# Edge tiles gathered once each, dense layers between the last steps of a segment sum, on one core of a Trainium2 chip

## The chip, the cores and the metric

The kernel runs on one NeuronCore of a Trainium2 chip (trn2). A core has five engines with an instruction queue each: TensorE (PE, with its weight loads as PEld) for matrix products, VectorE (DVE) and ScalarE (ACT) for elementwise work, GpSimd (POOL), which here issues the indirect DMAs, and SyncE (SP), which issues plain DMAs. The metric is the device time of one execution in microseconds. Before the change it is 7244.13 us, the median of 3 runs (7237.43 to 7245.76).

## The reference, cut to what matters

A graph of 6250 nodes with 128 features and 100000 edges, sorted by destination `dst`, goes through four blocks, each a layer norm, a graph layer and a residual:

```python
msg = h[src] * norm[:, None]                        # block 1: three GCN layers, ReLU after each
out = jax.ops.segment_sum(msg, dst, num_segments=n) + b
# norm = dis[src] * ew * dis[dst], dis = rsqrt(degree), self loops added to the edges

agg = segment_sum(edge_weight[:, None] * x[src], dst); out = x + agg    # block 2 (GIN)
h = relu(out @ W1 + b1);  return h @ W2 + b2

score = (softmax_dst(qs*k) + softmax_dst(qd*k) + softmax_dst(qs*qd)) * distance ** lam  # block 3
h = segment_sum(score[..., None] * v[dst], dst);  leaky_relu(h @ Wo.T + bo)

agg = segment_sum(x[src], dst) / max(deg, 1)        # block 4 (SAGE)
out = agg @ W_l.T + b_l + x @ W_r.T;  return out / norm(out)
```

## The kernel before

**Tiles, blocks and steps.** The edges lie in `NT` = 782 tiles of 128. The nodes lie in `NB` = 49 blocks of 128, taken in `NGR` = 13 groups of up to four. A tile whose edges reach into several blocks must be summed once for each. The kernel makes a plan on the chip from `dst`: a list of steps, each a pair of a tile and a block. It has room for `NS` = 832 steps (782 + 48, rounded up to a multiple of 16). The plan (`plan_reg`) gives the block of each step, the first edge of its tile, and columns with a column for every step: `rel_col` (the place of each edge in its block), `ew_col` (its weight), `src_col` (its source node).

**A pass** is one segment sum over all edges. There are five: three for the GCN layers, one for GIN, one for SAGE. For each of the 832 steps:

- POOL (`gathers`, L627) issues an indirect DMA that fetches the 128 source rows of the step from a table in HBM into a slot of `gath_ring` (64 slots, slot = step modulo 64). From step 64 on, a slot is written again when the product that read it has signalled `freed`, which every eighth product does.
- DVE (`sums`) waits for a batch of four gathers, makes the one-hot matrix of the step (L1347: which edge goes to which node, times the weight) in `hot_ring`, and six steps later adds the product to the block (L1358). The block's place in `AGG` comes from a register that a load from `plan_reg` fills for 16 steps at a time. Each add waits for the one before it.
- PE (`products`) runs `KEEP_BUSY` = 3 products of no use to the result (L749, 128x512 bf16, on a bank of their own), waits for the one-hot matrix, and multiplies it by the gathered rows (L751, f32; the trace shows two matmuls for each). The products go round seven PSUM banks.

**Between the passes** stand dense layers (`dense`, PE): per group four transposes (L726), a copy of the turned group by ACT (L947, in `dense_copies`), four products with the weights (L740), and DVE's read of the result from PSUM (`drained`). Turn g+1 stands ahead of product g. Before GCN layers 1 and 2 DVE also multiplies the sums by `dis` and adds the bias (`bias_add`, L1056), and a turn waits for that. The result goes to `Y` (L1067), SP stores it group by group to the table in HBM, and POOL copies it to `AGG` (L591), where the next sums start from the nodes' own rows. The first gather of a pass waits until all 13 stores have landed. After the third pass DVE scales and biases (L1075), adds the residual (L1078) and does the next norm; after the fifth it multiplies the sums by `inv_cnt` (L1129), and finishes the rows (L1151, L1153, L1155, L1138, L1140), which SP stores to `out`.

**Attention** (block 3) stands between the fourth and fifth pass. It too takes the 832 steps, with gathers of its own (L609) from the same `src_col`. **The setup** of some 387 us makes the plan and columns: seven gathers of edge fields (L571), casts and masks on DVE, transposes (PE) and copies (L1254) into the columns, degrees.

## Time and profile before

| | before |
|---|---|
| median of 3 runs | 7244.13 us (7237.43 to 7245.76) |
| profiled execution, its own time | 7238.71 us |
| its span | 7236.9 us |
| granted TensorE clock, mean | 0.962 of full speed |
| PE busy | 5333.0 us (74%) |
| POOL busy | 5036.9 us (70%) |
| DVE busy | 3802.8 us (53%) |
| ACT busy | 1178.4 us (16%) |

The span is the time from the first to the last instruction; the execution's own time is 1.8 us longer. Busy shares are means over passes, dense stages, setup and attention, which have different limits. The clock is given as a share of 2.4 GHz: 1.00 is 2.4 GHz and 0.50 is 1.2 GHz. Issuing instructions and the small instructions that compute addresses from registers are not counted as busy. A row of the timeline may merge several instructions, and the time in it is then their common stretch.

### The profile page before, as it was taken

To read this page: it belongs to the slowest core of one execution; us is meant where nothing else is said; L and a number is where in the kernel's file an instruction comes from. 1 tells how busy PE (TensorE), PEld (TensorE's weight loads), DVE (VectorE), ACT (ScalarE), POOL (GpSimd) and SP (SyncE) were. 2 spreads that over 40 slices of the span, in tenths; PEclk is the share of its full clock that TensorE was granted. 3 is DMA by queue.
4 is the path that set the end of the run, shared out by engine and by line. 5 is a ranking of instruction groups with operands and counts; after the bars stand their busy time and mean duration, and the time that the engine had idled before them with its cause. 6 is when DMAs were issued, how large, how long until landed. Compare 5 with 4: busy or idle time off the path is not lost.

```text
span 7236.9 us, 99962 instructions
## 1 busy us (share of the span) xinstructions
PE 5333.0 (74%) x30048; PEld 3426.1 (47%) x30467; DVE 3802.8 (53%) x12655; ACT 1178.4 (16%) x3122; POOL 5036.9 (70%) x5072
## 2 busy tenths in 40 slices
PE   0677777777777777777667777779999984777776
PEld 0444444444444444444344444556666663444444
DVE  7934444444444434444544444468988987333335
ACT  0600000000000000000000000057777773000000
POOL 7067777677777677777567777657777761777774
PEclk9599999999999999999999999989999996999999
DMA  1022222222222222222222222146666650222221
GB/s 51 17 63 53 53 53 53 53 61 53 53 53 53 57 57 53 53 53 53 53 56 53 53 53 53 45 109 142 145 144 144 145 124 24 53 53 53 53 53 51
DMA packets 390629, 481.00 MB, mean 66 GB/s; under 512 B 106605, under 2 KB 292879, under 8 KB 390075
## 3 DMA queue, kind: packets, MB, share of 16 engines
q0 software_dynamic: 160528, 330.23, 18.3%
q1 hardware_dynamic: 226395, 143.05, 8.4%
q8 instruction: 244, 4.00, 0.2%
q14 instruction: 294, 2.41, 0.1%
q10 hardware_dynamic: 3168, 1.31, 0.1%
HBM read 449.69 MB, written 26.88 MB: 66 GB/s over the span
## 4 chain that ended last, share of the span: by engine, by line
POOL 56%; issue 20%; PE 10%; DVE 7%; DMA 5%; SPq 1%; ACT 1%; ACTq 0%; POOLq 0%; DVEq 0%
POOL pool L627 54%; DMA gath<-table,src_col 2%; DMA pool<-edge_attr 2%; DVE pool L1222 2%; POOL gath L609 2%; PE psum L660 1%; PE psum L792 1%; PE psum L783 1%; PE psum L776 1%; PE psum L818 1%; PE psum L740 1%; SPq L527 1%; PE psum L769 1%; PE psum L762 1%; DVE hot L1314 0%
## 5 line engine op out<-in xcount | busy, mean ns | idle before, releaser
L627 POOL DMA_INDIRECT pool<-table,src_col x4160 | 3932.9, 945 | 1439.2 <-issue 1266.3
L749 PE MATMUL psum<-busy_rows,iota_b 128*128 128x512 bf16 x12061 | 3303.3, 381 | 22.3 <-issue 0.4
L751 PE MATMUL psum<-pool 128*128 128x128 f32 x8320 | 1715.0, 288 | 1378.7 <-DVE pool L1347 1378.4
L751 PEld LDWEIGHTS psum<-pool 128*128 128x128 f32 x8320 | 1505.1, 191 | 2345.1 <-DVE pool L1347 1892.5
L1347 DVE TENSOR_SCALAR pool<-iota_f,rel_col,ew_col 128x128 f32<-128x128 f32 x3328 | 1242.1, 375 | 2289.7 <-DMA pool<-table,src_col 2288.7
L749 PEld LDWEIGHTS psum<-busy_rows,iota_b 128*128 128x128 bf16 x12480 | 1235.2, 99 | 546.0 <-issue 8.8
L1358 DVE TENSOR_TENSOR work<-work,psum 128x128 f32 x4160 | 1193.1, 287 | 251.9 <-PE psum L751 225.4
L609 POOL DMA_INDIRECT gath<-table,src_col x832 | 906.9, 1090 | 267.9 <-issue 220.4
L947 ACT ACTIVATE pool<-psum 128x512 f32<-128x512 f32 (+1 forms) x130 | 72.1, 566 | 4278.0 <-PE psum L726 4277.9
L1347 DVE TENSOR_SCALAR pool<-iota_f,rel_col 128x128 f32<-128x128 f32 x832 | 250.2, 302 | 577.9 <-DMA pool<-table,src_col 577.4
L818 PEld LDWEIGHTS psum<-pool,hot 128*128 128x128 f32 x1664 | 221.9, 198 | 120.4 <-issue 109.7
L783 PE MATMUL psum<-pool,weights 128*128 128x512 f32 x416 | 239.7, 659 | 0.0
L776 PE MATMUL psum<-pool 128*128 128x128 f32 x1664 | 234.9, 287 | 0.0
L792 PE MATMUL psum<-pool,head_sum 128*32 128x512 f32 x1248 | 233.3, 638 | 0.5 <-DVE pool L1379 0.5
L818 PE MATMUL psum<-pool,hot 128*128 128x72 f32 x1664 | 222.5, 276 | 8.8 <-DVE work L1443 5.7
L928 ACT ACTIVATE ln_rstd<-ln_rstd 128x4 f32<-128x4 f32 (+1 forms) x52 | 10.6, 204 | 1333.0 <-DVE ln_rstd L1321 1333.0
L776 PEld LDWEIGHTS psum<-pool 128*128 128x128 f32 x1664 | 216.2, 203 | 0.0
L1374 DVE TENSOR_TENSOR pool<-psum,pool 128x512 f32<-128x512 f32 x208 | 142.0, 683 | 128.6 <-PE psum L792 121.8
L769 PE MATMUL psum<-ident,gath 128*128 128x128 f32 x832 | 142.2, 282 | 69.2 <-DMA gath<-table,src_col 68.8
L964 ACT ACTIVATE pool<-QV 128x128 f32 x832 | 189.5, 298 | 12.7 <-DVE pool L1451 5.6
L740 PE MATMUL psum<-weights,pool 128*128 128x128 f32 x980 | 145.3, 298 | 45.4 <-ACT pool L947 44.3
L1377 DVE SCALAR_TENSOR_TENSOR pool<-psum,bk_col,pool 128x512 f32<-128x512 f32 x208 | 154.2, 741 | 27.2 <-PE psum L783 26.7
(195 smaller groups left out, 3769.2 us busy)
## 6 DMA issues: line engine op xcount, KB each, us to landing
pool<-table,src_col POOLq DMA_INDIRECT x4160, 2.5
pool<-edge_attr SPq DMA_DIRECT2D x832, 64.0 KB
pool<-step_masks SPq DMA_DIRECT2D x624, 48.0 KB
pool<-rel_rows SPq DMA_DIRECT2D x208, 128.0 KB
table<-work SPq DMA_DIRECT2D x60, 256.0 KB, 2.3
gath<-table,src_col POOLq DMA_INDIRECT x832
table<-QV SPq DMA_DIRECT2D x12, 256.0 KB, 2.3
out<-X SPq DMA_DIRECT2D x12, 256.0 KB
```

Of the source, the lines that this page charges most:

```text
L609: gp.indirect_dma_start(out=q_src[:, n % SLOTS, :], out_offset=None, in_=table[0][:, :], in_offset=bass.IndirectOffsetOnAxis(ap=src_col[:, ...
L627: gp.indirect_dma_start(out=gath_ring[:, s % RING, :], out_offset=None, in_=source[:, :], in_offset=bass.IndirectOffsetOnAxis(ap=src_col[: ...
L740: ins = pe.matmul(psum[:, 4 + g % 2, i * P:(i + 1) * P], tr[:, 2 * k + g % 2, i * P:(i + 1) * P], weights[:, WI[w], :], start=(k == 0), st ...
L749: pe.matmul(psum[:, SUM_BANKS, :], iota_b[:, :], busy_rows[:, :], start=True, stop=True)
L751: pe.matmul(psum[:, s % SUM_BANKS, 0:D], hot_ring[:, s % HOT_RING, :], gath_ring[:, s % RING, :], start=True, stop=True).then_inc(steps.pr ...
L769: pe.transpose(psum[:, B_QS, j * P:(j + 1) * P], q_src[:, n % SLOTS, :], ident[:, :]).then_inc(qsrc_turned, 1)
L776: pe.matmul(psum[:, B_QD, j * P:(j + 1) * P], q_block[:, n % SLOT2, :], expand[:, two, j * P:(j + 1) * P], start=True, stop=True).then_inc ...
L783: pe.matmul(psum[:, B_K, :], weights[:, WI["Wk"], :], attr_t[:, g % 2, :], start=True, stop=True).then_inc(keyed, 1)
L792: ins = pe.matmul(psum[32 * kind:32 * (kind + 1), bank, :], head_sum[:, q, :], prod[:, kind, :], start=(q == 0), stop=(q == QUADS - 1), ti ...
L818: ins = pe.matmul(psum[:, B_SUM, q * ACCW:(q + 1) * ACCW].rearrange("p (k i h) -> p k i h", k=3, i=KINDS), hot[:, two * QUADS + q, :], val ...
L1347: v.tensor_scalar(hot_ring[:, s % HOT_RING, :], iota_f[:, :], rel_col[:, s:s + 1], ew_col[:, s:s + 1] if weighted else None, ALU.is_equal, ...
L1358: v.tensor_tensor(into, into, psum[:, a % SUM_BANKS, 0:D].rearrange("p (a d) -> p a d", a=1), ALU.add).then_inc(steps.added, 1)
```

## The change

- `gathers` loops over the 782 tiles instead of the 832 steps, from a `src_col` that has a column for every tile. A step finds its tile's slot by a third row of the plan (tile modulo 64), from which PE loads registers for 16 steps at a time. DVE waits for tile s before step s, for the first 782 steps; the last 48 steps (`PS` = 830 steps are left) wait for no gather. A gather of tile t waits for the product of step t-13 (`slot_free`), and every fourth product signals `freed`.
- `KEEP_BUSY` is 2, and the last 48 steps have none.
- A block b is complete once 782 + b steps are added. So the turns and products of the dense layers of GCN 1 and 2, GIN 1 and SAGE stand between the last steps (`then`), a stage every four steps from step 788, and DVE's reads of them a read every four steps from step 796. After the third pass, DVE's residual and norm stand there from step 788. What is not through by the last step follows it.
- The last 48 steps use banks 7, 6, 2, 3 (SAGE: 7, 6), since the dense stages take the others. An add stands seven steps behind its one-hot matrix, four steps in the last 48 (SAGE: two).
- The add takes `dis` of the block (SAGE: `inv_cnt`) as a factor, in place of L1056, L1075's factor and L1129. The GCN biases of layers 0 and 1 are columns (`gcn_bias`) that ACT's copy of the turned group adds; the third is added in `gcn_out`.
- ACT, not POOL, sets `AGG` to the nodes' own rows, times `dis` (`gcn_start`: 49 activations of 128x128 a layer).
- The setup makes both layouts of the sources: three more loads, a cast, two more groups of transposes and copies, and two stores to HBM. SP loads the layout by steps before attention, and that by tiles after it.

```diff
-        FREE = 8
+        FREE = 4
-        KEEP_BUSY = 3
+        KEEP_BUSY = 2
...
+            def slot_free(self, t):
+                steps = t + FREE - 1 - RING + NB - 1 + 1
+                return self.nth * (PS // FREE) + ceil_div(steps, FREE) if steps > 0 else 0
+            def bank(self, s):
+                return s % SUM_BANKS if s < NT else self.tail_banks[(s - NT) % len(self.tail_banks)]
+            def lead(self, s):
+                return (SUM_BANKS if s < NT else len(self.tail_banks)) - 1
+            def group_added(self, g):
+                return self.before + NT + groups[g][1] - 1
+        passes = [Pass(i, (7, 6, 2, 3)) for i in range(4)] + [Pass(4, (7, 6))]
...
             for layer in range(3):
-                for g, (lo, hi) in enumerate(groups):
-                    gp.wait_ge(gcn[layer].drained, gcn[layer].before + g + 1)
-                    gp.tensor_copy(AGG[:, lo:hi, :], Y[:, lo:hi, :]).then_inc(gcn_started, 1)
                 gathers(gp, layer, table[layer % 2], passes[layer])
...
-            for s in range(NS):
-                if s % FREE == 0 and s >= RING:
-                    gp.wait_ge(steps.freed, (steps.before + s - RING) // FREE + 1)
+            for t in range(NT):
+                if t % FREE == 0 and t >= RING - NB:
+                    gp.wait_ge(steps.freed, steps.slot_free(t))
                 gp.indirect_dma_start(
...
+            dense(pe, gcn[0], [AGG], ["W0"], lambda g: pe.wait_ge(norm_x.normed, norm_x.before + g + 1))
+            products(pe, passes[0], dense_stages(pe, gcn[1], [AGG], ["W1"], complete(passes[0])))
+            products(pe, passes[1], dense_stages(pe, gcn[2], [AGG], ["W2"], complete(passes[1])))
+            products(pe, passes[2])
+            products(pe, passes[3], dense_stages(pe, gin_1, [AGG], ["G1"], complete(passes[3])))
...
+            products(pe, passes[4], dense_stages(pe, sage_dense, [AGG, Y], ["Wl", "Wr"], complete(passes[4])))
...
+            def stage_at(k):
+                if k < NGR:
+                    turn(k)
+                if k >= 1:
+                    multiply(k - 1)
...
+            for s in range(PS):
+                if s % REGS == 0:
+                    slots = load_plan(mybir.EngineType.PE, 2, s, REGS, RING - 1, "the plan takes the tile modulo RING")
+                if s < NT:
+                    for _ in range(KEEP_BUSY):
+                        pe.matmul(psum[:, SUM_BANKS, :], iota_b[:, :], busy_rows[:, :], start=True, stop=True)
                 pe.wait_ge(steps.hot, steps.before + s + 1)
...
+                          gath_ring[:, bass.ds(slots[s % REGS], 1), :].rearrange("p a d -> p (a d)"), start=True,
                           stop=True).then_inc(steps.product(s)[0], 1)
+                if then and s >= NT + STAGE_AT and (s - NT - STAGE_AT) % GROUP == 0:
+                    then.pop(0)()
...
+            def gcn_start(layer, g):
+                act.wait_ge(gcn[layer].drained, gcn[layer].before + g + 1)
+                for b in range(lo, hi):
+                    ins = act.activation(AGG[:, b, :], Y[:, b, :], ACT.Copy, scale=dis[:, b:b + 1])
...
+            def gcn_out(g):
+                v.wait_ge(passes[2].added, passes[2].group_added(g))
+                v.tensor_tensor(AGG[:, lo:hi, :], AGG[:, lo:hi, :], bias_of("b2", hi - lo), ALU.add)
...
+            for s in range(PS + SUM_BANKS):
+                while added < PS and (s >= PS or added < s - steps.lead(s)):
...
+                        v.scalar_tensor_tensor(into, part, scale[:, bass.ds(blocks[added % REGS], 1)], into, ALU.mult,
+                                               ALU.add).then_inc(steps.added, 1)
+                    added += 1
+                if s < PS:
+                    if s < NT and s % BATCH == 0:
+                        v.wait_ge(batch_here[s // BATCH % NBATCH], batch_value(steps.nth, s))
...
+                    if s >= NT + then_at and (s - NT - then_at) % GROUP == 0:
+                        then(groups_done)
+                        groups_done += 1
+            for g in range(groups_done, NGR):
+                then(g)
```

The order of the instructions shows three places. First DVE at the end of the first pass, before: the last adds (L1358; "ISA" computes the block's address from the register and carries the waits), then scale and bias (L1056) and the reads of the dense products (L1067).

```order
L1358 ISA [waits pass_added,pass_freed]
L1358 TENSOR_TENSOR work<-work,psum 128x128
L1056 SCALAR_TENSOR_TENSOR work<-work,dis,bias 128x128 [waits pass_added]
L1056 SCALAR_TENSOR_TENSOR work<-work,dis,bias 128x128 x11
L1067 TENSOR_TENSOR work<-psum,dis 128x512 [waits dense_multiplied]
L1056 SCALAR_TENSOR_TENSOR work<-work,dis,bias 128x128 x4
L1067 TENSOR_TENSOR work<-psum,dis 128x512 [waits dense_multiplied]
```

The same place now: four adds in a row where the last 48 steps begin, then an add (L1446) and a one-hot matrix (L1452) in turn, and after each four such pairs a read of a dense product (L1151).

```order
L1446 ISA [waits pass_added,pass_multiplied]
L1446 SCALAR_TENSOR_TENSOR work<-psum,dis,work 128x128
L1446 ISA [waits pass_added,pass_multiplied]
L1446 SCALAR_TENSOR_TENSOR work<-psum,dis,work 128x128
L1452 TENSOR_SCALAR pool<-iota_f,rel_col,ew_col 128x128
...
L1452 TENSOR_SCALAR pool<-iota_f,rel_col,ew_col 128x128
L1151 TENSOR_TENSOR work<-psum,dis 128x512 [waits dense_multiplied]
L1446 ISA [waits pass_added,pass_multiplied]
L1446 SCALAR_TENSOR_TENSOR work<-psum,dis,work 128x128
L1452 TENSOR_SCALAR pool<-iota_f,rel_col,ew_col 128x128
```

L1056 is gone, and L1151, which is the old L1067, stands between steps. Second PE, in the last steps of the first pass, before: fillers (L749), product (L751), then the dense layer's turns (L726) and products (L740).

```order
L749 MATMUL psum<-busy_rows,iota_b 128x512 x3
L751 MATMUL psum<-pool 128x128 [waits pass_hot]
L726 MATMUL psum<-ident,work 128x128 [waits gcn_biased]
L726 MATMUL psum<-ident,work 128x128 x3
L726 MATMUL psum<-ident,work 128x128 [waits gcn_biased]
L726 MATMUL psum<-ident,work 128x128 x3
L740 MATMUL psum<-weights,pool 128x128 [waits dense_drained,dense_copied]
L740 MATMUL psum<-weights,pool 128x128 x3
```

And now, from the last step with fillers (L824) on; L826 is the product, whose slot comes from a register, L788 the turn and L800 the dense product.

```order
L824 MATMUL psum<-busy_rows,iota_b 128x512 x2
L826 ISA [waits pass_hot]
L826 MATMUL psum<-pool 128x128
L826 ISA [waits pass_hot]
L826 MATMUL psum<-pool 128x128
...
L788 MATMUL psum<-ident,work 128x128 [waits dense_copied,pass_added]
L788 MATMUL psum<-ident,work 128x128 x3
L800 MATMUL psum<-weights,pool 128x128 [waits dense_copied]
L800 MATMUL psum<-weights,pool 128x128 x3
L826 ISA [waits pass_hot]
L826 MATMUL psum<-pool 128x128
```

A stage of the dense layer now stands behind every fourth product, and a product behind it waits for the stage. Third POOL, in the piece of the difference that holds the first passes:

```order
-L591 COPY work<-work 128x512 x12
-L591 COPY work<-work 128x128
-L627 DMA pool<-table,src_col 128x128 x832
-L591 COPY work<-work 128x512 x12
-L591 COPY work<-work 128x128
-L627 DMA pool<-table,src_col 128x128 x1664
+L685 DMA pool<-table,src_col 128x128 x3128
```

The copies are gone, and four passes now have 3128 = 4 x 782 gathers in one row.

## Rows read from the trace of the kernel before

**Rows 1.** The page: the chain that ended last, shares of the span.
```profile
POOL 56%; issue 20%; PE 10%; DVE 7%; DMA 5%; SPq 1%; ACT 1%; ACTq 0%; POOLq 0%; DVEq 0%
```

**Rows 2.** The page, groups by line: count, busy us, mean ns, idle before.
```profile
L627 POOL DMA_INDIRECT pool<-table,src_col x4160 | 3932.9, 945 | 1439.2 <-issue 1266.3 <-DMA table<-work 172.9
...
L1358 DVE TENSOR_TENSOR work<-work,psum 128x128 f32 x4160 | 1193.1, 287 | 251.9 <-PE psum L751 225.4 <-issue 11.9 <-DVE work L1358 6.2
```

**Rows 3.** Timeline of POOL, passes' ends and starts: start, us, instruction, idle before.
```profile
1426.39 0.94 POOL L627 DMA_INDIRECT pool<-table,src_col  x1 [0.30 <-issue]
...
1463.53 0.97 POOL L627 DMA_INDIRECT pool<-table,src_col  x1 [1.91 <-DMA table<-work]
...
2539.88 0.97 POOL L627 DMA_INDIRECT pool<-table,src_col  x1 [2.19 <-DMA table<-work]
...
3635.06 0.94 POOL L627 DMA_INDIRECT pool<-table,src_col  x1 [55.54 <-DMA table<-work]
...
7166.77 0.94 POOL L627 DMA_INDIRECT pool<-table,src_col  x1 [0.30 <-issue]
```

**Rows 4.** Timeline within one batch of four steps, DVE and PE.
```profile
909.80 0.34 DVE L1347 TENSOR_SCALAR pool<-iota_f,rel_col,ew_col 128x128 f32<-128x128 f32 x1
...
910.22 0.38 PE L751 MATMUL psum<-pool 128*128 128x128 f32 x2
...
910.30 0.34 DVE L1347 TENSOR_SCALAR pool<-iota_f,rel_col,ew_col 128x128 f32<-128x128 f32 x1
...
911.09 0.39 PE L751 MATMUL psum<-pool 128*128 128x128 f32 x2
```

**Rows 5.** Timeline of the first pass's last batch, and of the dense layer's end.
```profile
1429.05 0.35 DVE L1347 TENSOR_SCALAR pool<-iota_f,rel_col,ew_col 128x128 f32<-128x128 f32 x1 [3.03 <-DMA pool<-table,src_col]
...
1429.45 0.49 PE L751 MATMUL psum<-pool 128*128 128x128 f32 x2 [1.34 <-DVE pool L1347]
...
1434.15 0.29 DVE L1358 TENSOR_TENSOR work<-work,psum 128x128 f32 x1 [0.21 <-DVE work L1358]
...
1457.43 0.66 PE L726 MATMUL psum<-ident,work 128*128 128x128 f32 x4 [0.45 <-DVE work L1056]
```

**Rows 6.** Timeline: GIN's second layer starts; SAGE's first group.
```profile
4699.67 1.04 PE L726 MATMUL psum<-ident,work 128*128 128x128 f32 x8
...
7180.47 1.04 PE L726 MATMUL psum<-ident,work 128*128 128x128 f32 x8
7180.67 0.69 DVE L1151 TENSOR_TENSOR pool<-psum,bias 128x512 f32<-128x512 f32 x1 [4.16 <-PE psum L740]
7181.34 1.95 PE L740 MATMUL psum<-weights,pool 128*128 128x128 f32 x16
```

**Rows 7.** Groups by form, of what the change moves or alters.
```profile
L934 ACT ACTIVATE work<-X,ln_shift,ln_rstd 128x128 f32<-128x128 f32 x196 | 79.4, 481 | 2.5
...
L871 ACT ACTIVATE weights<-psum 128x128 f32<-128x128 f32 x6 | 1.7, 278 | 4.2 <-PE psum L695 4.2
...
L1056 DVE SCALAR_TENSOR_TENSOR work<-work,dis,bias 128x128 f32<-128x128 f32 x98 | 33.8, 407 | 0.1
L1067 DVE TENSOR_TENSOR work<-psum,dis 128x512 f32<-128x512 f32 x36 | 24.7, 686 | 21.0 <-PE psum L740 20.9
...
L1075 DVE SCALAR_TENSOR_TENSOR work<-work,dis,bias 128x128 f32<-128x128 f32 x49 | 14.0, 347 | 0.0
```

**Rows 8.** Timeline of PE where a batch came late in the first pass.
```profile
914.90 0.68 PE L751 MATMUL psum<-pool 128*128 128x128 f32 x2 [1.91 <-DVE pool L1347]
...
916.65 0.63 PE L751 MATMUL psum<-pool 128*128 128x128 f32 x2
```

**Rows 9.** Windows: stretch, length, busy us of PE PEld DVE ACT POOL, PEclk, DMA.
```profile
912.00:914.00 2.00, 0.99 (x6) 0.36 (x4) 0.00 (x0) 0.00 (x0) 1.39 (x3) 1.00 0.15 43
...
916.00:918.00 2.00, 2.00 (x8) 1.05 (x6) 0.54 (x4) 0.00 (x0) 1.43 (x2) 0.50 0.18 45
```

**Rows 10.** Timeline of the setup's longest step and of the first dense layer.
```profile
68.44 124.00 DVE L1222 TENSOR_SCALAR pool<-pool,base_of 128x128 f32<-128x128 f32 x7
...
209.31 1.15 DVE L1254 CAST src_col<-psum 128x512 int32<-128x512 f32 x2
...
373.41 0.69 DVE L1067 TENSOR_TENSOR work<-psum,dis 128x512 f32<-128x512 f32 x1 [0.64 <-PE psum L740]
```

More of the change, by code:

```diff
@@ L424, in build @@
         REGS = 16
+        STAGE_AT = 6
+        DRAIN_AT = 14
         def sync(sp):
@@ L727, in turn, with multiply @@
                     ins.then_inc(d.turned, 1)
-            turn(0)
-            for g, (lo, hi) in enumerate(groups):
-                if g + 1 < NGR:
-                    turn(g + 1)
+            def multiply(g):
+                lo, hi = groups[g]
                 pe.wait_ge(d.copied, d.before + (g + 1) * K)
@@ L1122, in vector @@
             settle()
-            sums(v, 4, passes[4], False)
-            def mean(g):
-                lo, hi = groups[g]
-                if g == 0:
-                    v.wait_ge(passes[4].added, passes[4].before + NS)
-                v.tensor_tensor(AGG[:, lo:hi, :], AGG[:, lo:hi, :], col_bc(inv_cnt, lo, hi), ALU.mult).then_inc(mean_made, 1)
             def result(g):
@@ L1140, in result, with sage_drain @@
                 v.tensor_tensor(X[:, lo:hi, :], X[:, lo:hi, :], st, ALU.add).then_inc(result_made, 1)
-            mean(0)
-            mean(1)
-            for g, (lo, hi) in enumerate(groups):
+            def sage_drain(g):
+                lo, hi = groups[g]
                 n = hi - lo
@@ L1159, in vector @@
                     result(g - 1)
-            result(NGR - 1)
+                if g == NGR - 1:
+                    result(g)
+            sums(v, passes[4], None, inv_cnt, DRAIN_AT, sage_drain)
         def product_of(g):
@@ L1338, in norm_feed, with sums @@
                 norm_end(v, norm, g)
[L1340 removed]
+        def sums(v, steps, weight, scale, then_at, then):
             v.wait_ge(plan_loaded, 16)
[L1343 to L1359 removed]
@@ new lines, in sums @@
+            added, groups_done = 0, 0
+            for s in range(PS + SUM_BANKS):
+                while added < PS and (s >= PS or added < s - steps.lead(s)):
+                    if added % REGS == 0:
+                        blocks = load_blocks(mybir.EngineType.DVE, added, REGS)
+                    v.wait_ge(*steps.product(added))
+                    if added >= 1:
+                        v.wait_ge(steps.added, steps.before + added)
+                    into = AGG[:, bass.ds(blocks[added % REGS], 1), :]
+                    part = psum[:, steps.bank(added), 0:D].rearrange("p (a d) -> p a d", a=1)
+                    if scale is None:
+                        v.tensor_tensor(into, into, part, ALU.add).then_inc(steps.added, 1)
+                    else:
+                        v.scalar_tensor_tensor(into, part, scale[:, bass.ds(blocks[added % REGS], 1)], into, ALU.mult,
[4 more added lines that the diff above has]
+                        v.wait_ge(batch_here[s // BATCH % NBATCH], batch_value(steps.nth, s))
+                    v.tensor_scalar(hot_ring[:, s % HOT_RING, :], iota_f[:, :], rel_col[:, s:s + 1],
+                                    weight[:, s:s + 1] if weight is not None else None, ALU.is_equal,
+                                    ALU.mult if weight is not None else ALU.bypass).then_inc(steps.hot, 1)
+                    if s >= NT + then_at and (s - NT - then_at) % GROUP == 0:
+                        then(groups_done)
+                        groups_done += 1
```

198 lines of the change are left out of this document (110 added, 88 removed).

## The prediction, made before the changed kernel was timed

> **What bounds the kernel now.** I read the chain of waits first. Its largest share is POOL, with "issue" behind it [rows 1]. The groups by line say what that is: 4160 gathers of 0.945 us, and 1266 us in which POOL waited for nothing but its own next issue, 0.30 us for each [rows 2]. So a gather costs 1.25 us, and a pass is 832 x 1.25 = 1040 us of them. DVE's adds wait on PE and its one-hot matrices on the gathers; neither sets the pace: within a batch DVE needs 0.50 us for a pair of matrix and add, and PE, at full clock with three fillers, 0.87 us a step [rows 4].
>
> POOL's timeline then shows what lies between passes [rows 3]. The first pass's last gather ends at 1427.33, and the next pass starts at 1463.53: a gap of 36.2 us. Pass 2 is like it (start to start 1076.3 us). After pass 3 the gap is 55.5 us. Pass 4's last gather should end at 3635.06 + 1040 = 4675.1, and what comes next there, GIN's second layer, starts at 4699.67 [rows 6], 24.6 us later. After the last gather of all (7167.71) 69.2 us remain of the span of 7236.9 us.
>
> The sum is made against the profiled execution, 7238.7 us; its span is 1.8 us shorter, and the median of the runs is 5.4 us longer, 0.07%.
>
> **Removed: 50 gathers a pass.** 50 x 1.25 = 62.5 us, five times: 312 us. They are steps whose tile is there already, and two of padding. Attention keeps its 832.
>
> **Added: 48 steps after the last gather.** They did lie under gathers; now they lie behind them. From the last gather's end:
> - 1.7 us until the first one-hot matrix of the last batch (1427.33 to 1429.05 [rows 5]).
> - Two pairs, 1.1 us. Then four adds in a row where one stood, since an add now follows by four steps and not seven: three more at 0.50 us, which is what chained adds take (0.29 + 0.21 of waiting for the last one [rows 5]), 1.5 us.
> - 48 pairs. The pair was 0.50 us [rows 4]. The add becomes a scalar_tensor_tensor with a factor read through a register. That form took 0.407 and 0.347 us on other operands [rows 7], against the add's 0.287 [rows 2], so a pair lies between 0.50 and 0.62 us. I take 0.55, nearer to the pair that was seen: 26.4 us.
> - Three more chained adds at the end, 1.5 us.
>
> Together 32.2 us a pass.
>
> **Moved: the dense layers of GCN 1 and 2.** Nine of 13 reads stand between the steps, at 0.69 us [rows 7]: 6.2 us. A PE stage is four turns and four products, 0.66 us [rows 5] and about 1.1 us, and the four step products 0.2 us each (0.87 less three fillers of 0.215). That is 2.6 us, against DVE's 4 x 0.55 + 0.69 = 2.9 us for the same four steps. PE just fits under DVE, but each waits for the other once a group; I allow 0.3 us of the waiting each time, 2.7 us (bounds 0 and 1.5 us each). The last groups stay uncovered: from the last full turn at 1457.43 to the first gather of the next pass at 1463.53 took 6.1 us [rows 3, 5]; with ACT's new work in between I take 6.5. The first stages run at half clock (below), 2.5 us. Sum 32.2 + 6.2 + 2.7 + 6.5 + 2.5 = 50.1 us where 62.5 + 36.2 = 98.7 us were: **48.6 us less, twice**.
>
> **GIN's first layer**: the same, without ACT's rows and the store at the end, 47.1 us where 62.5 + 24.6 = 87.1 us were: **40 us less**.
>
> **After pass 3** DVE bounds the gap before and now. Of its 55.5 us the first 7.1 are the adds' end (to 1434.44 in the first pass [rows 5]), and 48.4 the residual, norm and store. The factor goes into the add, so that per group a plain bias add of 0.69 us stands for four of 0.347 us with their starts overlapped: 5 us less over 12 groups. 32.2 + 43.4 = 75.6 us where 118.0 were: **42 us less**. PE is not needed in that stretch but for products.
>
> **SAGE.** Two banks, so an add follows its matrix by two: matrix to product 0.40 us, product 0.49 [rows 5], then add 0.25; a pair can't be under 0.60 us. 48 x 0.60 = 28.8; ahead of them 1.7 + 1.1 + 6 chained adds, 3.0. PE's stages are 1.04 + 1.95 us [rows 6] and lie beside DVE's 3.9 us of work a group, but for the first two: 5 us. DVE's own work is that from 7180.67 to the end, 56.2 us [rows 6], less 11 of the multiplications by `inv_cnt` at the 0.69 us of that form [rows 7], 48.6 us. Half clock 2.5 us. Sum 90.7 us where 62.5 + 69.2 = 131.7 us were: **41 us less**.
>
> **Setup.** DVE's cast of the second layout stands ahead of L1222, whose 124 us end at 192.4 whatever comes before [rows 10]: hidden. Two more copies of a column group are on the path, 1.1 us [rows 10]. The stores and loads of the layouts are waited for long after they land. In the first dense layer ACT gets four activations a group beside the copy of 0.6 us. They take 0.278 us (plain copy) to 0.481 us (with two column operands) [rows 7]; at 0.35 us ACT's period is 2.0 us, and the layer's was 1.33 us (0.69 + 0.64 of waiting [rows 10]). So ACT bounds this layer: 0.67 x 11 = **7.5 us more** (bounds 2 and 14). That POOL no longer copies gives nothing: the gathers wait for the stores.
>
> Sum: 2 x 48.6 + 40 + 42 + 41 = 220 us less, 8.6 us more: 7238.7 - 211.6 = 7027 us; with half of what the median lies above, **7030 us**.
>
> **The clock with two fillers.** A batch is 5.0 us of gathers. PE's work in it was 4 x 0.87 = 3.5 us and becomes 4 x 0.65 = 2.6 us, so that it idles some 2.4 us in each (two fillers of the next step run ahead of the wait). In the trace one batch came late and PE idled 1.91 us [rows 8]; the clock, 1.00 till then, was 0.50 right after and steps took 1.75 us until it came back [rows 8, 9]. So I expect 0.50 for part of every batch, and a mean well under 0.96. At 0.50 a step with two fillers is 1.75 - 0.43 = 1.32 us, a batch 5.3 us: PE is then never idle, and the clock comes back as it did here. The gathers wait for a product 13 tiles back, 16.2 us, and that product is through some 2.5 + 5.3 us after its gather was issued. The pass keeps its 1.25 us; only the tails start slow, which is in the sum with 2.5 us each. The Trainium skill, page "TensorE: Matmul & The Clock Gate", section "HAM oscillation — how this bites in real kernels", has the rule: where short bursts of matmuls alternate with waits for transfers, the clock falls in each wait and every burst starts cold. By it the sum stands; without it the four terms of 2.5 us would go and the time be 7020 us. The trace agrees, by that one late batch.
>
> **Rivals.**
> - *The last steps are bound by handshakes.* Every step is matrix, product, add across two engines, PE's stages stand in its queue before products that DVE waits for, and each product has a register instruction ahead of it that carries the wait. If a group costs the sum of both engines' work rather than the longer, 1.5 to 2 us come on 9 groups in three passes and 3 us on 9 in SAGE, and pairs go to 0.7 us: 45 + 27 + 36 = 108 us, 7138 us. For it: chained adds show 0.21 us of pure waiting [rows 5]. Against: four matrices are always ahead.
> - *PE becomes the bound, slower than before.* If PE stayed at 0.50, with 1.32 us a step and the register instruction on top, the 3910 steps would cost more than their gathers. The point from which this decides is 211.6 / 3910 = 0.054 us over 1.25: a mean step above 1.304 us is slower than before. At 1.38 us: 3910 x 0.13 = 508 us more, 7535 us. For it: two fillers, and 1.32 is above that point. Against: in the trace continuous work brought the clock back within two steps or so, and a PE that bounds is continuously busy.
> - *The ring stalls the gathers.* The lead was 64 tiles and is 13. Late batches and a slow PE could meet in it. Against: 16.2 us against 7.8. If a twentieth of a microsecond a gather came of it, 195 us, nearly all would be gone: 7225 us, with both signs about; a milder form, a third of that, gives 7095 us.
> - That the change doesn't do what it says is excluded by the order: 782 gathers a pass.
>
> **How the numbers follow.** Forecast 0.80, handshakes 0.11, PE bound 0.04, ring 0.05. The bounds: pair 0.50 to 0.62, waiting 0 to 1.5 us, ACT 2 to 14 us, half clock 0 to 5 us a tail give about 45 us below and 60 us above; toward the handshakes the range goes on somewhat: 6985 to 7105 us. A measurement of this kernel tells 0.2%, 14 us, from no change. Faster: the forecast, the handshakes, and most of the ring, 0.94; same 0.01; slower 0.05.
>
> **What would show it.** Right: the gathers at 1.25 us still, 782 of them a pass, and a start to start of some 1028 us (1076.3 now) in the first two passes and 1053 us (1095.2) in the third; no wait of POOL for PE; a mean clock clearly below 0.962; the first dense layer's reads 2.0 us apart. Wrong: gathers that wait for products; adds in the last steps over 0.7 us apart; a PE that has no idle time within the batches.

## The result, and the profile after

The changed kernel takes 7045.85 us (median of 4 runs, 7039.36 to 7051.43) where the kernel before, on the same chip, takes 7244.94 us (4 runs, 7237.43 to 7245.95): ratio 0.9727, 95% interval [0.971, 0.9744]. Forecast were 7030 us in a range of 6985 to 7105. The profiled execution took 7039.36 us, with a span of 7037.6 us and a mean granted clock of 0.87 (0.962 before).

The page of the kernel after: the chain of waits, then groups by line. They answer to [rows 1, 2].

```profile
POOL 47%; issue 19%; PE 13%; DVE 9%; DMA 8%; SPq 2%; ACT 1%; DVEq 1%; ACTq 0%; POOLq 0%
```

```profile
L685 POOL DMA_INDIRECT pool<-table,src_col x3910 | 3697.8, 946 | 1638.3 <-issue 1149.8
...
L1446 DVE SCALAR_TENSOR_TENSOR work<-psum,dis,work 128x128 f32 x2490 | 870.4, 350 | 140.3 <-PE psum L826 114.3
```

There are 3910 gathers of 0.946 us for 4160 of 0.945, still 0.30 us apart: the pace is the same and 250 are gone. Most of the idle time before them that "issue" did not end lies where the passes begin. The add with the factor takes 0.350 us; GIN, which has no factor, keeps the plain add of 0.287. The timeline of POOL shows the new gaps, against those of [rows 3].

```profile
1417.23 0.95 POOL L685 DMA_INDIRECT pool<-table,src_col  x1 [48.15 <-DMA table<-work]
...
2443.32 0.94 POOL L685 DMA_INDIRECT pool<-table,src_col  x1 [49.33 <-DMA table<-work]
...
3502.29 0.94 POOL L685 DMA_INDIRECT pool<-table,src_col  x1 [81.56 <-DMA table<-work]
```

The first gather of all starts at 392.16, so that start to start the first three passes take 1025.1, 1026.1 and 1059.0 us; 1028 us for the first two and 1053 us for the third were forecast, and before they took 1076.3 and 1095.2 us. The same readings for each part of the span, in us:

| part | before | after | change | forecast |
|---|---|---|---|---|
| setup, to the first gather | 387.2 | 392.2 | +4.9 | +8.6 |
| gathers of the five passes | 5199.2 | 4887.8 | -311.4 | -312 |
| gap after pass 1 | 36.2 | 48.2 | +12.0 | +13.9 |
| gap after pass 2 | 36.3 | 49.3 | +13.1 | +13.9 |
| gap after pass 3 | 55.6 | 81.6 | +26.0 | +20.1 |
| pass 4's end to attention | 70.8 | 88.0 | +17.2 | +22.5 |
| attention, to the first gather of pass 5 | 1382.5 | 1395.5 | +13.0 | 0 |
| SAGE, last gather to the end | 69.2 | 95.1 | +25.9 | +21.5 |

Without attention the span changes by -212.3 us, and -211.6 was forecast. The 13.0 us of attention were not forecast, and are most of what the median lies above 7030. The table compares one trace with one: before_again, below, is a second trace of the kernel before, with a setup of 391.5 us and an attention of 1393.1 us, so part of those two rows is variation.

The waits of POOL (what, releaser: us in all, times, longest) show that the ring held: a gather that waits for a product does so for 0.3 us, which is what it would have waited for its issue.

```profile
POOL pool L685 <- issue: 1149.8, 3773, 0.3
...
POOL pool L685 <- PE psum L826: 40.2, 132, 0.3
```

A window of a pass (length; PE, PEld, DVE, ACT, POOL busy; then the clock) shows the lower clock. Microsecond by microsecond it is 0.50 from 1000 to 1002 and from 1010 to 1012 us, and 1.00 from 1003 to 1009 and from 1013 us on: it falls after some of the waits within the batches, not after all. DVE's timeline of the first dense layer shows that its reads are 1.65 us apart, where 2.0 was forecast and 1.33 was before [rows 10].

```profile
1000.00:1020.00 20.00, 15.32 (x69) 9.56 (x68) 9.55 (x34) 0.00 (x0) 15.12 (x17) 0.85 0.22 55
```

```profile
377.12 0.69 DVE L1151 TENSOR_TENSOR work<-psum,dis 128x512 f32<-128x512 f32 x1 [0.90 <-PE psum L800]
378.77 0.69 DVE L1151 TENSOR_TENSOR work<-psum,dis 128x512 f32<-128x512 f32 x1 [0.96 <-PE psum L800]
```

### The profile page after: what moved, and what is told of

Read it like the earlier page. It is cut to its first block, busy times and chain, and to the rows that moved or that the text cites. A ratio compares the mean times of both kernels' runs of the same rounds, so it can differ in the third digit from the quotient of the medians.

```text
span 7037.6 us, 95131 instructions
## 1 busy us (share of the span) xinstructions
PE 5024.6 (71%) x25794; PEld 3266.4 (46%) x25794; DVE 4005.6 (57%) x12494; ACT 1222.8 (17%) x3269; POOL 4769.8 (68%) x4783
## 4 chain that ended last, share of the span: by engine, by line
POOL 47%; issue 19%; PE 13%; DVE 9%; DMA 8%; SPq 2%; ACT 1%; DVEq 1%; ACTq 0%; POOLq 0%
POOL pool L685 47%; DMA pool<-table,src_col 3%; DMA pool<-edge_attr 3%; DVE work L1308 2%; DVE work L1446 2%; PE psum L872 2%; PE psum L863 2%; PE psum L856 2%; PE psum L718 1%; PE psum L826 1%; PE psum L898 1%; SPq L584 1%; PE psum L800 1%; DMA gath<-table,src_col 1%; PE psum L842 1%
## 5 line engine op out<-in xcount | busy, mean ns | idle before, releaser
L685 POOL DMA_INDIRECT pool<-table,src_col x3910 | 3697.8, 946 | 1638.3 <-issue 1149.8
L826 PE MATMUL psum<-pool 128*128 x8300 | 1966.0, 326 | 1468.2 <-DVE pool L1452 1457.4
L826 PEld LDWEIGHTS psum<-pool 128*128 128x128 f32 x8300 | 1711.0, 223 | 2699.5 <-issue 2419.7
L824 PE MATMUL psum<-busy_rows,iota_b 128*128 128x512 bf16 x7820 | 2767.3, 441 | 67.8 <-issue 67.7
L1452 DVE TENSOR_SCALAR pool<-iota_f,rel_col,ew_col 128x128 f32<-128x128 f32 x3320 | 1243.6, 376 | 1967.4 <-DMA pool<-table,src_col 1966.4
L664 POOL DMA_INDIRECT gath<-table,src_col x832 | 898.8, 1080 | 287.6 <-issue 220.9
L1446 DVE SCALAR_TENSOR_TENSOR work<-psum,dis,work 128x128 f32 x2490 | 870.4, 350 | 140.3 <-PE psum L826 114.3
L824 PEld LDWEIGHTS psum<-busy_rows,iota_b 128*128 128x128 bf16 x7820 | 863.6, 112 | 183.6 <-issue 90.3
L1452 DVE TENSOR_SCALAR pool<-iota_f,rel_col 128x128 f32<-128x128 f32 x830 | 264.8, 320 | 484.1 <-DMA pool<-table,src_col 484.1
L1044 ACT ACTIVATE pool<-psum,gcn_bias 128x512 f32<-128x512 f32 (+1 forms) x26 | 17.2, 661 | 2005.7 <-PE psum L788 2005.7
L1446 DVE SCALAR_TENSOR_TENSOR work<-psum,inv_cnt,work 128x128 f32 x830 | 291.1, 351 | 73.0 <-PE psum L826 44.9
L1444 DVE TENSOR_TENSOR work<-work,psum 128x128 f32 x830 | 238.0, 287 | 48.4 <-PE psum L826 40.1
L856 PE MATMUL psum<-pool 128*128 128x128 f32 x1664 | 240.4, 292 | 0.0
L856 PEld LDWEIGHTS psum<-pool 128*128 128x128 f32 x1664 | 222.6, 208 | 0.0
L842 PE MATMUL psum<-ident,pool 128*128 128x128 f32 x832 | 150.5, 289 | 64.5 <-DMA pool<-edge_attr 61.0
```

The source lines that it names most:

```text
L664: gp.indirect_dma_start(out=q_src[:, n % SLOTS, :], out_offset=None, in_=table[0][:, :], in_offset=bass.IndirectOffsetOnAxis(ap=src_col[:, ...
L685: gp.indirect_dma_start(out=gath_ring[:, t % RING, :], out_offset=None, in_=source[:, :], in_offset=bass.IndirectOffsetOnAxis(ap=src_col[: ...
L824: pe.matmul(psum[:, SUM_BANKS, :], iota_b[:, :], busy_rows[:, :], start=True, stop=True)
L826: pe.matmul(psum[:, steps.bank(s), 0:D], hot_ring[:, s % HOT_RING, :], gath_ring[:, bass.ds(slots[s % REGS], 1), :].rearrange("p a d -> p ...
L842: pe.transpose(psum[:, B_ATTR, j * P:(j + 1) * P], attr[:, n % SLOT2, :], ident[:, :]).then_inc(attr_turned, 1)
L856: pe.matmul(psum[:, B_QD, j * P:(j + 1) * P], q_block[:, n % SLOT2, :], expand[:, two, j * P:(j + 1) * P], start=True, stop=True).then_inc ...
```

## The experiments

Twelve kernels ran, in three sets of four, each set on one chip with the kernel before beside it. Gaps are in the order of the table: after pass 1, 2, 3, 4, and SAGE's end. The gathers of a pass take 977 to 979 us in all kernels but two: before_again, with its 832 a pass, takes 1039 to 1040 us, and ring5 is told below.

| kernel | median us (runs) | ratio to before | clock | gaps | attention |
|---|---|---|---|---|---|
| keep3 | 7040.4 | 0.9723 [0.9707, 0.9739] | 0.954 | 49.4, 49.0, 81.6, 86.7, 93.6 | 1392.0 |
| fixed_slot | 7039.9 | 0.9714 [0.9692, 0.9736] | 0.861 | 48.1, 49.0, 81.5, 87.1, 91.9 | 1409.1 |
| apart | 7091.7 | 0.9788 [0.9763, 0.9812] | 0.863 | 60.9, 60.5, 80.3, 94.2, 103.3 | 1414.5 |
| fill_p2 | 7041.0 | 0.9717 [0.9701, 0.9733] | 0.872 | 48.8, 49.2, 81.5, 87.0, 95.7 | 1399.7 |
| before_again | 7244.3 (10) | 0.9999 [0.9989, 1.0009] | 0.960 | 36.8, 36.9, 55.5, 71.1, 69.4 | 1393.1 |
| dram_last | 7025.1 (4) | 0.9696 [0.9678, 0.9714] | 0.872 | 48.2, 48.0, 81.5, 86.8, 93.5 | 1381.0 |
| keep0 | 7044.4 (4) | 0.9726 [0.971, 0.9743] | 0.613 | 48.1, 48.8, 81.6, 86.2, 94.2 | 1399.1 |
| ring5 | 7541.3 (4) | 1.0411 [1.0394, 1.0429] | 0.836 | 48.7, 48.4, 81.6, 87.6, 93.3 | 1406.0 |
| after_again | 7049.0 (5) | 0.9737 [0.9723, 0.975] | 0.870 | 49.2, 49.4, 81.5, 87.8, 93.6 | 1398.7 |
| dram_again | 7030.2 (5) | 0.9704 [0.9691, 0.9717] | 0.873 | 47.9, 49.5, 81.5, 87.0, 93.2 | 1387.9 |
| lead2 | 7078.7 (4) | 0.9777 [0.9762, 0.9792] | 0.872 | 58.1, 58.4, 88.1, 97.2, 93.7 | 1388.7 |
| ring9 | 7036.2 (4) | 0.9713 [0.9698, 0.9728] | 0.871 | 49.1, 49.3, 81.5, 86.6, 96.9 | 1409.6 |

### The clock: keep3, keep0 and fill_p2

keep3 sets back the fillers, keep0 has none, and fill_p2 adds one in the last 40 steps of the third pass alone:

```diff
-        KEEP_BUSY = 2
+        KEEP_BUSY = 3        # keep3;  0 in keep0
```

```diff
+                if steps.nth == 2 and s >= NT + 8:
+                    pe.matmul(psum[:, 5, :], iota_b[:, :], busy_rows[:, :], start=True, stop=True)
```

> The changed kernel with three fillers a step again instead of two. Theory A (the clock falls to 0.50 in the idle part of every batch, and that is what makes the last steps start slow): the mean granted clock rises from 0.87 to above 0.93, the gathers stay 1.25 us apart, and the five stretches behind the last gathers get 0 to 3 us shorter each, 7036 to 7046 us in all. Theory B (the register instruction ahead of each product is what costs): the clock rises too, but nothing gets shorter. If the fillers were the bound, PE at 0.65 us a step would have had room that 0.87 has not, and POOL would now wait for PE.

> The kernel after without any filler product (the multiplications that only keep TensorE busy). My prediction's theory: the clock doesn't matter in the passes so long as a step at half clock is under a gather's 1.25 us; without fillers the clock's mean falls far under 0.87, to 0.5 to 0.6, a step costs 0.5 to 0.9 us at half clock, and the 782 gathers of a pass still take 977 to 979 us. The tails pay: pairs there need a product of 0.2 us at full clock and 0.4 us at half clock under DVE's 0.59, which still hides it, and the stages between the steps get longer than DVE's work; I expect 5 to 15 us a stretch in four of the five, and dense work in attention 10 to 40 us longer: 7070 to 7120 us. The rival (the clock is what holds the passes at their pace): the gather loops get longer than 985 us and wait for products, total over 7200 us.

> The changed kernel with one filler (bank 5) ahead of each product in the last 40 steps of the third pass only. Theory A (half clock): DVE's waits of 0.80 us for a product there go, and the stretch of 81.6 us falls to 75 to 78 us; total 4 to 6 us less. Theory B (register): the stretch stays within 1 us or grows, as the filler stands before the product.

With three fillers the clock is back at 0.954, and no gap changes by more than some 1.5 us. Without any it stands at 0.50 throughout the passes (mean 0.613), and still none changes by more than 1.8 us; after_again, with nothing changed, differs by up to 1.5 us. The windows of keep0, in a pass and at the start of the last steps, show why the passes don't care: PE is busy for 10.55 of 20 us there, at half clock, and DVE and POOL as before. In the last steps the clock stays at 0.50 for the first 12 us, to about 1381.5, and is 1.00 after that.

```profile
1000.00:1020.00 20.00, 10.55 (x34) 8.05 (x33) 9.59 (x34) 0.00 (x0) 15.12 (x17) 0.50 0.21 53
...
1380.00:1395.00 15.00, 13.29 (x103) 12.36 (x102) 13.81 (x45) 7.58 (x19) 0.00 (x0) 0.95 0.20 59
```

In the last steps after pass 3, which have no dense stages, the clock stays low in all of these kernels: from 3430 to 3470 us it is 0.50 in the kernel after and in keep0, 0.52 in keep3, and DVE is busy for some 37 of the 40 us all the same. So my theory that a low clock costs nothing under the gathers is shown, at its lowest too.

The terms of 2.5 us for a cold start are refuted after passes 1, 2 and 4: keep0, whose last steps start cold and stay so for 12 us, has gaps as short as the others. keep3 alone would not show it, for its clock falls to 0.50 in the first pass's last steps too (1377.5 to 1381.5 us); behind pass 4 it stays at 1.00, where the kernel after falls to 0.50, and the gap is 86.7 us against 88.0 (87.8 in after_again). My 5 to 15 us a gap for keep0 were as wrong: DVE sets the pace of these steps. The fourth term, SAGE's, stays open. There the clock falls to 0.50 or stays at it early in the last steps in every variant, keep3 included, and no run held it up. fill_p2 changes nothing either, 81.50 us for 81.57, but it tells little: its clock from 3430 to 3470 us is only 0.62, against 0.50.

### The register: fixed_slot

Products read slot s modulo 64, by a constant, so that other rows are summed than the plan names:

```diff
-                if s % REGS == 0:
-                    slots = load_plan(mybir.EngineType.PE, 2, s, REGS, RING - 1, "the plan takes the tile modulo RING")
...
-                          gath_ring[:, bass.ds(slots[s % REGS], 1), :].rearrange("p a d -> p (a d)"), start=True,
+                          gath_ring[:, s % RING, :], start=True,
```

> The changed kernel, but the products read slot (step modulo 64) instead of the slot of the step's tile, so that neither the register nor its load stands on PE; what it sums is other rows than the reference's. Theory B (register instruction ahead of each product): a product follows its one-hot matrix sooner, SAGE's stretch from the last gather to the end, 96.9 us, falls by 5 us or more, and the stretch after the third pass, 81.6 us, by 3 us or more. Theory A (half clock): both stay within 2 us.

Four gaps change by under 1 us, SAGE's by 3.2. The slot's registers cost next to nothing; in SAGE, whose add follows its product closely, it may be up to 3 us, where that gap varies by 3.7 us (93.2 to 96.9) among the runs that left it as it is. The gain of some 6 us in the median is within what the intervals leave open.

### What interleaving is worth: apart

```diff
-        STAGE_AT = 6
-        DRAIN_AT = 14
+        STAGE_AT = 60
+        DRAIN_AT = 60
```

> The changed kernel with no dense stage and no read between the last 48 steps; all of them follow the last step. It prices the interleaving alone. By the prediction's terms the stretches after passes 1, 2 and 4 grow by 12 to 14 us each (nine groups of some 1.65 us of ACT's and PE's work come out from under DVE's steps, less the reads' waits), the one after pass 3 stays (DVE bounds it either way), and SAGE's grows by 3 us: +41 us, 7087 us. By the rival of handshakes the interleaving gives nothing in SAGE or costs there: its stretch gets shorter by 5 us or more.

The gaps change by +12.7, +11.2, -1.3, +6.3 and +8.2 us, 37 in all where 41 were expected. The total changes by 46, but 19 us more of attention stand in this trace, a stretch that the edit leaves alone. So of the 212 us the stages between the last steps bring 37, and the other 175 are the gathers taken away, less what the 48 steps cost behind them. Two parts were off: GIN's gap was to grow by 12 to 14 us, and SAGE's by 3. After pass 3 the work is DVE's either way, and interleaving it costs 1 us. In SAGE the rival of handshakes asked for a gap shorter by 5 us or more, and it got longer by 8.2.

### The lead of SAGE's adds: lead2

```diff
-        passes = [Pass(i, (7, 6, 2, 3)) for i in range(4)] + [Pass(4, (7, 6))]
+        passes = [Pass(i, (7, 6)) for i in range(4)] + [Pass(4, (7, 6))]
```

> The kernel after, but the sums of the last 48 steps alternate between two PSUM banks in all passes, as SAGE's already do, where four took turns. An add then follows its matrix by two steps, not four. In the trace of the kernel after a pair of matrix and add took 0.587 us with four banks (after pass 3) and about 0.83 us in SAGE's tail. Theory A (the lead of two is what makes SAGE's pairs slow: matrix to product, product, add in a chain): the stretch after pass 3 gets 40 to 48 pairs x 0.24 = 10 to 12 us longer (81.6 to 92), the first two and GIN's 8 to 20 us each, since the stages then stand in the chain too, in all 35 to 60 us: 7080 to 7105 us. Theory B (SAGE's pairs are slow by the slower clock or by its stages, and the lead is hidden): the stretch after pass 3 stays within 2 us of 81.6, total under 7055 us. SAGE itself doesn't change (95 us).

The gap after pass 3 grows by 6.6 us, 0.14 us for each of 48 pairs, not 0.24; those after passes 1, 2 and 4 by 9 to 10 us. So the lead of two makes pairs longer, and by more where dense stages stand in the chain as well. Theory A holds in direction, but just under the lower edge of its total (7078.7 us, 7080 to 7105 expected) and short of it after pass 3. That SAGE's own pairs would be as fast as the others' with four banks was not tried.

### The ring: ring5 and ring9

```diff
-                steps = t + FREE - 1 - RING + NB - 1 + 1
+                steps = t + FREE - 1 - RING + NB - 1 + 1 + 8      # ring5;  + 4 in ring9
```

> The kernel after with each gather waiting for a product eight tiles later than it has to: a lead of 5 tiles (6.2 us) where there were 13 (16.2 us). Adds and DRAM layouts are unchanged. My prediction's sum: a product is through 2.5 + 5.3 us after its gather was issued at half clock, and 2.5 + 3.5 us and less at full clock, so 6.2 us is just where the wait begins to bite: some batches stall by up to 1.5 us. If a tenth of the 195 batches of a pass do so for 1 us, 20 us a pass, 100 us in all: 7145 us, bounds 7045 (never) and 7700 (each batch 0.7 us). If the total stays at 7045 us, the lead has much more room than I reckoned; if the passes double their stall, the rival of the ring was nearer than its 0.05 said. The trace's waits of POOL for products tell it: 132 of 0.3 us each with 13 tiles, and they stand there in place of the issue.

> The kernel after with each gather waiting for a product four tiles later than it has to: a lead of 9 tiles (11.2 us) where there were 13 (16.2 us) and ring5 had 5 (6.2 us; its passes took 1075 to 1083 us of gathers for 977, total 7541 us). By my prediction's sum, a product is through 7.8 us after its gather was issued at half clock, so a lead of 11.2 us has no stall: 977 to 979 us a pass, total 7045 us. The rival (late batches and the queue of gathers add to that; the lead of 13 is just enough): some stall, 5 to 40 us a pass, total 7070 to 7250 us.

With a lead of 9 tiles nothing changes. With 5 the gathers of the first four passes take 1075 to 1084 us, the fifth's 1064, and the total lies 298 us over the kernel before. The waits of POOL for PE in ring5:

```profile
POOL pool L685 <- PE psum L826: 639.5, 470, 2.3
```

These are 470 waits of 1.36 us (639.5 / 470), of which 0.30 is what the issue takes anyway, for some 975 batches: about every second one stalled, by a microsecond on average, where I had put a tenth of them; the 100 us expected became 495. My 7.8 us from a gather to the end of its product lie between the two leads, 6.2 and 11.2 us, and where the stall begins does too. So the 13 tiles had 4 or more to spare.

### Attention: before_again, dram_last, after_again, dram_again

before_again and after_again are the two kernels unchanged. dram_last and dram_again are one kernel, with two declarations moved:

```diff
-        src_steps = nc.dram_tensor("src_steps", [P, SRW], I32).ap()
-        src_tiles = nc.dram_tensor("src_tiles", [P, SRW], I32).ap()
         att_flat = nc.dram_tensor("att_flat", [E], F32).ap()
...
         table = [nc.dram_tensor(f"table{i}", [NP, D], F32).ap() for i in range(2)]
+        src_steps = nc.dram_tensor("src_steps", [P, SRW], I32).ap()
+        src_tiles = nc.dram_tensor("src_tiles", [P, SRW], I32).ap()
```

> The kernel before, unchanged, once more with a trace: a control for attention. The stretch from pass 4's end to the first gather of pass 5 took 1382.5 us in the profiled execution before and 1395.5 in the one after, 1392.0 to 1414.5 in four variants of the kernel after. Theory A (the change makes attention slower, by something in the program): this run shows 1382 to 1386 us, its gathers loop 1170 us long. Theory B (attention varies from execution to execution, whatever the program): it lies anywhere from 1380 to 1410 us, and the 13 us that my prediction didn't have are no effect of the change. Either way the median is 7245 us and the ratio 1.000.

> The kernel after, with the two new layouts in DRAM declared behind the node table, so that the table, the attention sums' layouts and the masks lie where they lay in the kernel before. Nothing else differs. Theory A1 (attention's gathers and loads got slower by where their tensors lie in DRAM): attention goes from 1395.5 back to 1382 us and the total to about 7030 us. Theory A2 (it comes from what the program does elsewhere, or from how the instructions are laid out) and theory B (plain variation): attention stays between 1390 and 1415 us, the total 7040 to 7050 us. Passes and stretches between them as in the kernel after, within 1 us.

> The kernel after, unchanged, once more, beside dram_again on the same chip. Median 7045 us (7035 to 7052), ratio to before 0.9727. Its attention shows how far that stretch varies with nothing changed: the kernel before gave 1382.5 and 1393.1 us in two traces, the after 1395.5 in one. Theory A (the placement in DRAM costs it): 1390 us or more again, and gathers that wait for TensorE 60 us in all. Theory B (plain variation): anywhere from 1380 to 1410 us.

> The kernel after with the two new layouts behind the node table in DRAM, a second time, in more rounds. The first time it took 7025 us (ratio 0.9696 [0.9678, 0.9714]) where the kernel after has 7046 (0.9727 [0.971, 0.9744]), and attention took 1381.0 us. Theory A (the placement decides): 7025 us within 6, ratio under 0.9710, attention 1378 to 1386 us, at least 10 us under after_again in the medians. Theory B (variation from execution to execution): 7040 to 7047 us, no difference from after_again that its interval tells from none.

Both theories hold a part. The kernel before gives 1382.5 and 1393.1 us for attention in two traces with nothing changed, so one pair of traces can't tell 13 us. But the medians can: dram_again takes 7030.2 us and after_again 7049.0 on one chip, with intervals that don't meet (0.9704 [0.9691, 0.9717] and 0.9737 [0.9723, 0.975]). In the set before that, dram_last stood at 0.9696 [0.9678, 0.9714] and keep0, with the layouts ahead, at 0.9726 [0.971, 0.9743] on one chip. The size is less sure than the direction. Seven kernels with the layouts ahead and nothing else of weight changed (after, after_again, keep3, keep0, fixed_slot, fill_p2, ring9) have medians of 7036.2 to 7049.0 us, against 7025.1 and 7030.2, and the interval of ring9 on the same chip, [0.9698, 0.9728], does meet that of dram_again.

Attention takes 1381.0 and 1387.9 us with the layouts behind the tables; with them ahead, ten traces give 1388.7 to 1414.5, mean 1401. The other parts of these kernels are the same: gaps and gathers agree within 1.5 us. POOL's waits for the turns of the gathered rows (L664, released by L849), over the whole span, first of after_again, then of dram_again:

```profile
POOL gath L664 <- PE psum L849: 71.9, 123, 2.6
```

```profile
POOL gath L664 <- PE psum L849: 46.3, 100, 2.2
```

The gathers wait for TensorE 26 us longer, and TensorE for the edges' attributes (L842) 20 us longer (63.4 and 42.9 us). That is how a long attention looks, and not a mark of the place: in the kernel before, which has no such layouts, the same two waits are 44.3 and 25.9 us in the first trace and 64.3 and 48.8 us in before_again. That the place of tensors in DRAM costs time here is shown by the medians, some 0.2 to 0.3%; through which tensor and by what mechanism isn't. It is also the version that beats both kernels: 7030.2 us.

## Why the prediction was right

- **Gathers, -312 us.** Right: 3910 at 1.25 us.
- **The last 48 steps.** The pair with the factor takes 0.587 us, not 0.55, and a chained add 0.587 (0.35 + 0.24), not 0.50. The last batch after pass 3, on DVE's timeline:

```profile
3423.79 0.35 DVE L1446 SCALAR_TENSOR_TENSOR work<-psum,dis,work 128x128 f32 x1 [0.24 <-DVE work L1446]
...
3424.96 0.35 DVE L1446 SCALAR_TENSOR_TENSOR work<-psum,dis,work 128x128 f32 x1 [0.24 <-DVE work L1446]
3425.23 0.34 DVE L1452 TENSOR_SCALAR pool<-iota_f,rel_col,ew_col 128x128 f32<-128x128 f32 x1
3425.55 0.35 DVE L1446 SCALAR_TENSOR_TENSOR work<-psum,dis,work 128x128 f32 x1
```

  In GIN, without the factor, the pair is 0.50 us as before. So the form with the factor costs 0.087 us more a pair; against the forecast it is 48 x 0.037 + 6 x 0.087 = 2.3 us a gap.
- **After pass 3, 75.6 forecast, 81.6 measured.** The term that failed. 2.3 us are the above. Some 2.4 us are a wait that the forecast had not: every 16th add comes 0.80 us late, here and at 3429.31 and 3475.11.

```profile
3452.05 0.35 DVE L1446 SCALAR_TENSOR_TENSOR work<-psum,dis,work 128x128 f32 x1 [0.80 <-PE psum L826]
```

  The profile names PE, but the product of this add is that of four matrices back, from the group before, and the wait is as long in fixed_slot, where PE loads no registers, and in keep0. What falls on each 16th add is DVE's own load of 16 block numbers (`load_blocks`). The kernel before has the same wait, every 20 us, that is every 16 gathers (the next is at 920.95, of 0.83 us):

```profile
900.91 0.29 DVE L1358 TENSOR_TENSOR work<-work,psum 128x128 f32 x1 [0.84 <-PE psum L751]
```

  There a gather's pace hid it; behind the last gather it is on the path, three times a pass. By its place it is the load; no run took the load away. The remaining 1.3 us stay unexplained.
- **GCN gaps, 50.1 forecast, 48.2 and 49.3 measured; GIN 5.3 us better.** Right by errors that met, which is luck. DVE's timeline of the first pass's last steps gives the split: the add before the first of the 48 pairs, an add that waits for a load, the add of the last pair, and the last add.

```profile
1373.27 0.35 DVE L1446 SCALAR_TENSOR_TENSOR work<-psum,dis,work 128x128 f32 x1 [0.24 <-DVE work L1446]
...
1389.42 0.35 DVE L1446 SCALAR_TENSOR_TENSOR work<-psum,dis,work 128x128 f32 x1 [1.11 <-PE psum L826]
...
1409.49 0.35 DVE L1446 SCALAR_TENSOR_TENSOR work<-psum,dis,work 128x128 f32 x1
...
1411.25 0.35 DVE L1446 SCALAR_TENSOR_TENSOR work<-psum,dis,work 128x128 f32 x1 [0.24 <-DVE work L1446]
```

  The 48 pairs and nine reads take 36.2 us, and 35.3 was forecast. Of them 28.2 are the pairs, 3.1 the three loads (0.8 us, and 1.1 us twice in this tail), and 4.9 are left for the reads, where 6.2 and another 2.7 of waiting between the engines were forecast. From the last add's end to the next gather (1417.23) pass 5.6 us, not 6.5. So pairs, chained adds and loads cost 5.4 us more than forecast, and the reads 1.3, the waiting 2.7, the end 0.9 and the half clock 2.5 us less. For GIN I took over the pair of 0.55 us though it has no factor; its 0.50 us pay there for most of the loads. Four pairs and a read take 2.87 us (reads at 1389.94 and 1392.81), where 2.9 was forecast: the stages do fit beneath.
- **SAGE, 90.7 forecast, 95.1 measured.** The floor of 0.60 us a pair was a floor: with two banks adds wait for PE again and again, by 0.2 to 0.9 us, and at the first two stages by 1.59 and 2.34 us.

```profile
6963.08 0.35 DVE L1446 SCALAR_TENSOR_TENSOR work<-psum,inv_cnt,work 128x128 f32 x1 [2.34 <-PE psum L826]
```

  For the two stages 5 us were forecast. The clock may count here: two pairs take 1.66 us at 0.50 (adds at 6953.40 and 6955.06) and 1.39 us at 1.00 (6966.51 and 6967.90), but that is a reading and not a test. lead2 shows what the lead of two costs elsewhere, 0.14 us a pair.
- **Setup, +8.6 forecast, +4.9 measured.** ACT's activation took 0.391 us and not 0.35, yet its period is 1.65 us and not 2.0: I had added four full durations to the copy, and activations that follow each other overlap in part (four take 1.27 us together), as the adds of DVE do. That makes 11 x 0.32 = 3.5 us in place of 7.5. The second trace of the kernel before has a setup of 391.5 us, so the +4.9 itself is known only to some 4 us.
- **Attention, 0 forecast.** The miss that moved the total. I had looked at what the change issues and not at where its new tensors lie. How much of the 13 us is their place, and how much variation, this pair of traces can't tell.
- **The rivals.** Handshakes show only in SAGE. PE as the bound is refuted by the changed kernel itself: its gathers keep their pace, POOL waits for PE by no more than the 0.3 us of an issue, and its clock is 0.86 to 0.88 over long stretches of the passes. keep0 stays at 0.50 throughout with the same gathers, but without the fillers that made the rival's 1.32 us a step. The ring is refuted by ring9. The mean clock well under 0.962 came as forecast. The Trainium skill, page "TensorE: Matmul & The Clock Gate", section "HAM oscillation — how this bites in real kernels", has bursts between waits start cold. keep0 is that case, at 0.50, and where the gathers set the pace it cost nothing; with two fillers only some bursts start cold (mean 0.87).
- **The range.** The bounds that I listed add up to some 33 us below the forecast and 62 us above, not to 45 and 60. The measured time lies 16 us above the forecast, within either.

## What to carry to other kernels

Where a fetch's issue sets the pace, count the fetches and take the double ones out; what then lies behind the last one must be priced by what its engine takes uncovered, register loads included, which a slower pace had hidden. Before a filler or a higher clock is paid for, ask which engine ends the wait: here the clock could fall from 0.95 to 0.61 at no price that the medians show (7040.4 and 7044.4 us). In SAGE's last steps, where an add follows its product closely, its price stays open. And compare the stretch that a change doesn't touch too, with more than one execution: new tensors in DRAM, declared ahead of the others, went with 0.2 to 0.3% more time.

## What the runs showed of the hardware that was not expected

- With two declarations of 448 KB each ahead of the tables in DRAM a stage with 126 GB/s of traffic, attention, took 1401 us (mean of ten traces, 1388.7 to 1414.5), and 1386 us without them there (mean of four, 1381.0 to 1393.1).
- On DVE each 16th add comes 0.80 us late, and up to 1.11 us among dense stages, where 16 registers are loaded; the profile puts it down to PE.
- With three fillers the clock was 1.00 from 1000 to 1020 us, with two 0.85, with none 0.50; in keep0, in the pass that follows, PE idled 2.43 us before a batch's products:

```profile
1499.53 1.89 PE L826 MATMUL psum<-pool 128*128 x6 [2.43 <-DVE pool L1452]
```

- A scalar_tensor_tensor of 128x128 that reads PSUM takes 0.350 us and the tensor_tensor 0.287, but a chain or a pair gets longer by 0.087 us, more than the 0.063 between the two.
